# Feed-forward variances as one 512-column product; the inverse deviation by logarithm and exponential on ACT and a Newton step on DVE

## What is computed

```
def ffn_layer(x, g, bln, W1, b1, W2, b2):
    mu = x.mean(-1, keepdims=True)
    var = ((x - mu) ** 2).mean(-1, keepdims=True)
    xn = (x - mu) / jnp.sqrt(var + 1e-05) * g + bln
    hg = xn @ W1 + b1
    a, gate = jnp.split(hg, 2, -1)
    return a * jax.nn.gelu(gate, approximate=False) @ W2 + b2

for i in range(DEPTH):
    x = attn_layer(shift_tokens(x), Wqkv[i], q_scale[i], k_scale[i], Wo[i]) + x
    x = ffn_layer(shift_tokens(x), ln_g[i], ln_b[i], W1[i], b1[i], W2[i], b2[i]) + x
```

## Time and profile before

| | us |
|---|---|
| median of 3 executions (lowest, highest) | 3338.47 (3333.91, 3343.07) |
| the profiled execution, its own time | 3337.87 |
| its span on the core | 3336.1 |

### The profile page before, as it was taken

How to read it: one execution, slowest core, us unless ns; L and a number is a source line. 1 busy time by engine, 2 the same in 40 slices (tenths; PEclk the granted TensorE clock), 3 DMA queues, 4 the chain that set the end, 5 groups by cost and what they waited for, 6 DMA issues and landing times.

```text
span 3336.1 us, 149930 instructions
## 1 busy us (share of the span) xinstructions
PE 3156.5 (95%) x63424; PEld 2622.5 (79%) x63424; DVE 2650.9 (79%) x4403; ACT 2380.2 (71%) x4536; POOL 2592.1 (78%) x2894
## 2 busy tenths in 40 slices
PE   5999999999999999999779999999999999999997
PEld 4888888788888888888668878888888888888875
DVE  3888888888888888888558888888888888888884
ACT  4777777777777777777537777777777777777774
POOL 5987887888788878887349778878887888787773
PEclk8999999999999999999879999999999999999999
DMA  2221222221221222221112222222212212221211
GB/s 82 76 58 51 68 62 55 64 65 52 64 67 53 62 67 55 62 64 51 32 26 75 58 55 67 62 52 68 64 49 67 64 53 65 64 56 50 54 46 40
DMA packets 117857, 195.41 MB, mean 59 GB/s; under 512 B 23756, under 2 KB 36552, under 8 KB 117192
## 3 DMA queue, kind: packets, MB, share of 16 engines
q1 hardware_dynamic: 117192, 185.82, 20.8%
HBM read 33.71 MB, written 1.05 MB: 10 GB/s over the span
## 4 chain that ended last, share of the span: by engine, by line
PE 66%; DVE 13%; ACT 10%; issue 9%; DVEq 0%; ACTq 0%; POOL 0%; DMA 0%; POOLq 0%; SPq 0%
PE s_ps L925 11%; PE tr L969 9%; DVE ss_floor L721 7%; PE tr L938 6%; PE tr L866 5%; PE o_ps L954 4%; PE f_ps L1015 4%; ACT qt L544 4%; PE tr L868 2%; PE tr L867 2%; PE qk_ps L866 2%; PE qk_ps L867 2%; PE qk_ps L868 2%; PE tr L893 2%; PE tr L906 2%
## 5 line engine op out<-in xcount | busy, mean ns | idle before, releaser
L420 POOL TENSOR_TENSOR rotated<-rotated 128x1024 f32<-128x1024 f32 x384 | 916.2, 2386 | 28.8 <-DVE rotated L714 28.8
L426 POOL TENSOR_TENSOR prob<-prob,rden 128x512 f32<-128x512 f32 x384 | 435.7, 1135 | 464.8 <-DVE rden L746 464.2
L449 POOL TENSOR_TENSOR rotated<-rotated,rn 128x1024 f32<-128x1024 f32 x384 | 730.6, 1903 | 30.1
L708 DVE TENSOR_TENSOR rotated<-qk_ps,rot 128x1024 f32<-128x1024 f32 x384 | 470.0, 1224 | 211.7 <-ACT sq L528 208.1
L574 ACT ACTIVATE pt<-tr 128x512 f32<-128x512 f32 x384 | 229.3, 597 | 450.8 <-PE tr L938 450.8
L714 DVE TENSOR_TENSOR rotated<-qk_ps,rot 128x512 f32<-128x512 f32 x768 | 491.0, 681 | 0.0
L925 PEld LDWEIGHTS s_ps<-kt,qt 64*32 64x32 f32 x24576 | 360.8, 107 | 140.4 <-issue 124.4
L721 DVE TENSOR_REDUCE ss_floor<-sq 128x16 f32<-128x1024 f32 x384 | 464.1, 1209 | 0.4
L925 PE MATMUL s_ps<-kt,qt 64*32 64x64 f32 x24576 | 423.2, 218 | 0.3 <-issue 0.2
L528 ACT ACTIVATE sq<-qk_ps 128x1024 f32<-128x1024 f32 x384 | 388.0, 1010 | 26.3 <-PE qk_ps L868 25.7
L969 PE MATMUL tr<-ot,wo 128*128 128x128 f32 x3072 | 406.6, 275 | 0.0
(11 more groups left out here) (152 smaller groups left out, 6968.9 us busy)
## 6 DMA issues: line engine op xcount, KB each, us to landing
vs<-vn SPq DMA_DIRECT2D x384, 192.0 KB, 2.6
vs<-vtail SPq DMA_DIRECT2D x384, 64.0 KB, 2.0
vtail<-vn SPq DMA_DIRECT2D x384, 64.0 KB, 2.3
staging<-layer_wqkv_dram SPq DMA_DIRECT2D x72, 256.0 KB, 3.0
wo<-layer_wo_dram SPq DMA_DIRECT2D x12, 512.0 KB, 3.9
xs<-xa SPq DMA_DIRECT2D x48, 128.0 KB, 2.3
fs<-xa SPq DMA_DIRECT2D x48, 128.0 KB, 2.3
xs<-xa SPq DMA_DIRECT2D x48, 127.8 KB, 2.4
```

The source lines that it names most:

```text
L420: nc.gpsimd.tensor_tensor(rot_c[h], rot_c[h], rot_s[h], ALU.add).then_inc(rot_added, 1)
L426: nc.gpsimd.tensor_tensor(prob[h][:, :, :], prob[h][:, :, :], rden[h][:, :].unsqueeze(2).to_broadcast([P, 2 * PAIRS, KEYS]), ALU.mult).the ...
L449: nc.gpsimd.tensor_tensor(folded, folded, rn[:, :].unsqueeze(2).to_broadcast([P, 2 * UH, DH]), ALU.mult).then_inc(qkn_ready, 1)
L708: nc.vector.tensor_tensor(rot_c[h], src, part(0, 0, DH), ALU.mult)
```

## The change

The variance becomes one product of the 128x128 matrix of 1/128 with the 512 columns of squares, so that every partition holds the variance of every token and nothing has to be spread. ACT takes the logarithm of variance plus epsilon and the exponential of -1/2 of it, and squares this first value; DVE makes one Newton step with it and the scaling in three operations of 512 columns. The factor -0.5 of the step is folded into the copy `fd`. The new ACT work stands at the end of slot 5, the new DVE work in slot 6, and DVE's work of slots 5 and 7, POOL's power and PE's `spread` are gone. The similar code of the layer norm ahead of each stack stays.

```diff
--- before.py
+++ after.py
@@ -141,8 +141,8 @@
         fsq = sb("fsq", [P, SEQ])
         fn_hi = sb("fn_hi", [P, SEQ], F32R)
         fn_lo = sb("fn_lo", [P, SEQ], F32R)
-        var = sb("var", [P, TPS])
-        rstd = sb("rstd", [P, TPS])
+        eps = sb("eps", [P, 1])
+        frsq = sb("frsq", [P, SEQ])
         mac_var = sb("mac_var", [P, SEQS, TPS])
         mac_rstd = sb("mac_rstd", [P, SEQS, TPS])
         gate = [sb(f"gate{i}", [P, HS]) for i in range(3)]
@@ -219,9 +219,11 @@
         fsq_ready = sem("fsq_ready")
         fd_ready = sem("fd_ready")
         fvarp_ready = sem("fvarp_ready")
-        fvar_ready = sem("fvar_ready")
-        frstd_ready = sem("frstd_ready")
-        frb_ready = sem("frb_ready")
+        flog_ready = sem("flog_ready")
+        fguess_ready = sem("fguess_ready")
+        fguess_squared = sem("fguess_squared")
+        fscaled = sem("fscaled")
+        fresidue_ready = sem("fresidue_ready")
         fn_ready = sem("fn_ready")
         fn_hi_ready = sem("fn_hi_ready")
         fn_split = sem("fn_split")
@@ -378,12 +380,13 @@
 
         @block.gpsimd
         def _(pool):
-            for released in (rn_ready, rot_added, qkn_ready, probn_ready, w1_split, frstd_ready):
+            for released in (rn_ready, rot_added, qkn_ready, probn_ready, w1_split):
                 pool.sem_inc(released, ONE)
             for h in range(2):
                 nc.gpsimd.memset(vtail[h][:, :, :], 0.0).then_inc(zeros_ready, 1)
                 nc.gpsimd.memset(kt[h][:, :, :], 0.0).then_inc(zeros_ready, 1)
             nc.gpsimd.memset(three[:, :], 3.0)
+            nc.gpsimd.memset(eps[:, :], EPS)
             nc.gpsimd.memset(ss_floor[:, :, :], SQUARE_FLOOR)
             nc.gpsimd.memset(mean_mat[:, :], 1.0 / P).then_inc(zeros_ready, 1)
             nc.gpsimd.memset(minus_half[:, :], -0.5).then_inc(zeros_ready, 1)
@@ -467,9 +470,6 @@
                     if live(p, n + 1):
                         inverse_norms(n + 1)
                         normalise(n + 1)
-                    if (it := ffn_of(p, n, VAR_AT + 1)) is not None:
-                        pool.wait_ge(fvar_ready, ONE + it + 1)
-                        nc.gpsimd.tensor_tensor(rstd[:, :], var[:, :], minus_half[:, 0:TPS], ALU.pow).then_inc(frstd_ready, 1)
                     g, m = layer_slot(p, n)
                     if m == 11:
                         split_w1(g)
@@ -584,7 +584,16 @@
 
                 act.wait_ge(fcen_ready, ONE + it + 1)
                 nc.scalar.activation(fsq[:, :], f_ps[:, :], ACT.Square).then_inc(fsq_ready, 1)
-                nc.scalar.activation(fd[:, :], f_ps[:, :], ACT.Copy).then_inc(fd_ready, 1)
+                nc.scalar.activation(fd[:, :], f_ps[:, :], ACT.Copy, scale=-0.5).then_inc(fd_ready, 1)
+
+            def inverse_std(it):
+
+                act.wait_ge(fvarp_ready, ONE + it + 1)
+                nc.scalar.activation(fsq[:, :], f_ps[:, :], ACT.Ln, bias=eps[:, :]).then_inc(flog_ready, 1)
+                act.wait_ge(flog_ready, it + 1)
+                nc.scalar.activation(frsq[:, :], fsq[:, :], ACT.Exp, scale=-0.5).then_inc(fguess_ready, 1)
+                act.wait_ge(fguess_ready, it + 1)
+                nc.scalar.activation(fsq[:, :], frsq[:, :], ACT.Square).then_inc(fguess_squared, 1)
 
             def normed_high(it):
                 l = it // SEQS % DEPTH
@@ -642,6 +651,8 @@
                         tokens_high(it)
                     if (it := ffn_of(p, n, MEAN_AT)) is not None:
                         centred(it)
+                    if (it := ffn_of(p, n, VAR_AT + 1)) is not None:
+                        inverse_std(it)
                     if (it := ffn_of(p, n, NORM_AT)) is not None:
                         normed_high(it)
                     if (it := ffn_of(p, n, GATED_AT)) is not None:
@@ -665,7 +676,7 @@
         @block.vector
         def _(dve):
             for released in (summed, ss_ready, rot_parts, max_ready, dif_ready, rden_ready, y_added, xs_split,
-                             fvar_ready, fn_ready, fn_split, hid_ready, xa_ready):
+                             fresidue_ready, fscaled, fn_ready, fn_split, hid_ready, xa_ready):
                 dve.sem_inc(released, ONE)
             dve.wait_ge(consts_in, 48)
             dve.wait_ge(zeros_ready, 8)
@@ -753,14 +764,15 @@
                 cols = xa[:, s, t * P:(t + 1) * P]
                 nc.vector.tensor_tensor(cols, tr0[:, 0:P], cols, ALU.add).then_inc(y_added, 1)
 
-            def variance(it):
-                dve.wait_ge(fvarp_ready, ONE + it + 1)
-                nc.vector.tensor_scalar(var[:, :], f_ps[:, 0:TPS], EPS, None, ALU.add).then_inc(fvar_ready, 1)
-
-            def spread(it):
+            def scale_normed(it):
+
                 l = it // SEQS % DEPTH
-                dve.wait_ge(frb_ready, ONE + it + 1)
-                nc.vector.scalar_tensor_tensor(fd[:, :], fd[:, :], vecs[:, l, 0:1], f_ps[:, :], ALU.mult, ALU.mult).then_inc(fn_ready, 1)
+                dve.wait_ge(fguess_squared, it + 1)
+                nc.vector.scalar_tensor_tensor(fsq[:, :], f_ps[:, :], EPS, fsq[:, :], ALU.add, ALU.mult).then_inc(fresidue_ready, 1)
+                nc.vector.scalar_tensor_tensor(fd[:, :], fd[:, :], vecs[:, l, 0:1], frsq[:, :], ALU.mult, ALU.mult).then_inc(fscaled, 1)
+                dve.wait_ge(fresidue_ready, ONE + it + 1)
+                dve.wait_ge(fscaled, ONE + it + 1)
+                nc.vector.scalar_tensor_tensor(fd[:, :], fsq[:, :], 3.0, fd[:, :], ALU.subtract, ALU.mult).then_inc(fn_ready, 1)
 
             def normed_low(it):
                 l = it // SEQS % DEPTH
@@ -792,10 +804,8 @@
                         prob_sums(n - 1)
                     if (it := staged_for(p, n, 2)) is not None:
                         tokens_low(it)
-                    if (it := ffn_of(p, n, VAR_AT + 1)) is not None:
-                        variance(it)
-                    if (it := ffn_of(p, n, SPREAD_AT + 1)) is not None:
-                        spread(it)
+                    if (it := ffn_of(p, n, SPREAD_AT)) is not None:
+                        scale_normed(it)
                     if (it := ffn_of(p, n, NORM_AT + 1)) is not None:
                         normed_low(it)
                     if (it := ffn_of(p, n, ADD_AT)) is not None:
@@ -829,7 +839,7 @@
         @block.tensor
         def _(pe):
             for released in (qk_ready, v_ready, qtp_ready, ktp_ready, s_ready, ptp_ready, o_ready, y_ready, fcen_ready,
-                             fvarp_ready, frb_ready, gated_ps, fy_ready):
+                             fvarp_ready, gated_ps, fy_ready):
                 pe.sem_inc(released, ONE)
             pe.wait_ge(consts_in, 48)
             pe.wait_ge(consts_ready, 2)
@@ -977,16 +987,7 @@
 
             def variances(it):
                 pe.wait_ge(fd_ready, ONE + it + 1)
-                for c in range(TPS):
-                    last = nc.tensor.matmul(f_ps[:, c:c + 1], fsq[:, c * P:(c + 1) * P], mean_mat[:, 0:1], start=True, stop=True)
-                last.then_inc(fvarp_ready, 1)
-
-            def spread(it):
-                pe.wait_ge(frstd_ready, ONE + it + 1)
-                for c in range(TPS):
-                    last = nc.tensor.matmul(f_ps[:, c * P:(c + 1) * P], rstd[:, c:c + 1].to_broadcast([P, P]), ident[:, :],
-                                            start=True, stop=True)
-                last.then_inc(frb_ready, 1)
+                nc.tensor.matmul(f_ps[:, :], mean_mat[:, :], fsq[:, :], start=True, stop=True).then_inc(fvarp_ready, 1)
 
             def gated(p, n, it):
                 pe.wait_ge(fn_split, ONE + it + 1)
@@ -1042,8 +1043,6 @@
                         centre(it)
                     if (it := ffn_of(p, n, VAR_AT)) is not None:
                         variances(it)
-                    if (it := ffn_of(p, n, SPREAD_AT)) is not None:
-                        spread(it)
                     if (it := ffn_of(p, n, GATED_AT)) is not None:
                         gated(p, n, it)
                 if p == 0:
```

## The result

The changed kernel takes 3402.17 us (median of 4 executions, 3399.34 to 3405.45) against 3336.19 us for the kernel before with all its executions so far. The ratio is 1.0195, with a 95% interval of 1.0175 to 1.0215: slower by 66 us. The prediction had said 3401 us, by the mechanism that follows. The profiled execution has a span of 3398.5 us against 3336.1, 62.4 us more.

A forecast was written before the change was run, and what follows sets the result against it. A 7.10 us ring through PE, DVE and ACT bounds the kernel outside PE's heavy slots. 46 x 1.40 = 64.4, less 1 for the ends, gives +63 on 3337.87: 3401 us, forecast 3388 to 3412 (chance 0.50), 3350 to 3430 (0.81).

The forecast's parts named there:

- The ring of 7.10 us and PE's 6.75: Between V marks (value projection starts on PE): lap through PE, DVE, ACT 7.10 us; PE without feed-forward work 6.75.
- The variance product, slot 4: On PE, one 512-column product for four one-column products: between 0 and +0.07 us, booked as 0.
- ACT, slot 5 to 6: Three new ACT operations delay slot 6's exponential by 1.40 us, making V6 0.77 us late.
- DVE, slot 6 to 7: Three new DVE operations, one held up by POOL, delay the rotation; V6 to V7 takes 8.27 us.
- The blocking of DVE by POOL: Slot 6: DVE's second new operation stands still until POOL's L426 is done, taking about 1.1 us.
- the rival: Slot 6: no meeting of DVE and POOL, V7 +0.93 us, +42 us in all, 3380 us; chance 0.18.
- The steady part: V7 1.40 us late, and the delay stays: 46 x 1.40 = 64.4 us.
- The two ends: Stand-alone last feed-forward behind each stack, at the lower clock: about 5.7 us instead of 6.17, -0.5 us, twice.
- The new work fills idle time: Faster rival: ACT's idle time around slot 5's copy takes the new work; -42 us, 3296 us; chance 0.08.
- Only ACT's delay counts: Rival: DVE catches up in slot 6, V7 +0.23 us, +10 us in all, 3348 us; chance 0.12.
- The third falls behind `normalise`: Rival, slot 6: DVE's third operation loses nearly 1.9 us more to POOL's L449; +147 us, 3485 us; chance 0.04.
- Dearer operations: Rival: logarithm and exponential towards their upper bound, 0.3 to 0.6 us more on the path; 3415 to 3430 us; chance 0.08.

The follow-up runs named there:

- swap: Changed kernel with DVE's first two new operations in the other order, the one with two SBUF inputs first: 3385.04 us, ratio 1.0148.
- psum_step: Changed kernel with DVE's three operations rewritten through the PSUM bank, each reading at most one tile of SBUF: 3386.34 us, ratio 1.0151.
- spread_tokens: Changed kernel with ACT's logarithm and exponential before slot 5's copy, DVE's operations in PSUM form across slots 6 to 8, later feed-forward and token staging: 3304.95 us.
- act_only: Changed kernel without the Newton step: product and ACT's three operations kept, one 512-column DVE operation in slot 7: 3357.60 us, ratio 1.0068.
- neither: Changed kernel with the product only: ACT's three operations and the Newton step left out, inverse deviation a constant 1.0: 3312.57 us, ratio 0.9932.
- tokens_after: Changed kernel with only the token staging moved, ACT's `xs_hi` one slot later and DVE's `xs_lo` two: 3408.68 us, ratio 1.0213.

## Why the prediction was right

The bound. The ring of 7.10 us and PE's 6.75 were read from slots 5 and 6 of one sequence. The run with the product alone shows the ring from V5 to V8, three slots in a row, and rules out that PE's full saving comes out.

The variance product, slot 4: booked at 0 between 0 and +0.07; it was -0.04.

ACT, slot 5 to 6: 0.77 us forecast, 0.86 measured. The logarithm takes 0.68 and not the 0.60 of a copy out of PSUM; the exponential and the square take 0.64 and 0.63, where 0.63 and 0.60 were booked.

DVE, slot 6 to 7: 8.27 forecast, 8.26 measured. Inside, errors offset each other: the second operation took 1.20 instead of 1.12 and the third started 0.11 us behind it instead of 0.04; but the first took 0.64 instead of 0.70, and the third lost nothing to POOL where 0.1 was booked. The blocking of DVE by POOL is the step on which the choice between 3380 and 3401 hung, and both swap and psum_step confirm it: without DVE's wait the kernel is 17 or 16 us faster, where the rival had put 21.

The Trainium skill's rule (SBUF — State Buffer, Who interferes with whom) was the ground for it beside the earlier trace rows. By that rule alone swap should move the waiting from DVE to POOL, and the trace agrees: 0.70 for 1.20 us on DVE, 1.44 for 1.04 on POOL. The other rule of the Trainium skill, to optimise the most-contended engine first (Perfetto Trace Analysis, Identifying the Most-Contended Engine), gives the sign of the product alone (3312.57 us), not its size. For the whole change it gives the wrong sign (3402.17 us).

The steady part was then forecast at 1.40 us and came at 1.44, so 64 and 66 us. The two ends were wrong in sign: -0.5 us each was forecast, +0.24 and +0.23 measured. The failed step is the product's duration there, taken as 1.46 from the centre product; it took 2.07. The granted clock was 0.72 over that centre product (3305.3 to 3306.7 before) and 0.50, the lower level, over the new one (3370.1 to 3372.1), where PE had stood idle for 1.18 us ahead of it. That the total still fits within about 1 us is partly luck. Between the profiled executions the stretch between the stacks gave 4 us back, which the prediction did not have. And between the medians the change costs 66 us, not 63; but the sum stood on 3337.87, and the median before came down to 3336.19 with one more execution.

The side effects: the projection in slot 7 starts 1.08 us behind the output projection (1042.38 to 1043.46) instead of 0.81, which is the 0.2 us booked, ahead of the longer wait of 1.02 for `queries`. And `fn_lo` in slot 0 did become slower (1.11 us on average instead of 0.75) without a cost to the slot, as said. PE's busy time fell by 29 us and not by some 40; no run here separates the reasons.

The rivals fell as follows. "The new work fills idle time" needs gaps at the place where the work is put; there is enough idle time (spread_tokens), but not there. "Only ACT's delay counts" would give 7.10 for slot 6 to 7; it was 8.26. "The third falls behind `normalise`" did not happen: POOL's small operations were themselves held up. "Dearer operations" came to 0.08 us for the logarithm, 0.01 for the exponential and 0.03 for the square.

## What to carry to other kernels

In an in-order pipeline over several engines, follow one lap of the waits and compare it with the busiest engine's own work for that lap: if they are close, work moved off the busiest engine pays only until that engine's time falls to the lap's (here 7.64 - 7.10 = 0.54 of 0.89 us). Work put on the others then lengthens the lap, unless it stands where they already wait. Look for such gaps by place and length (here 1.0 us ahead of one copy on ACT, 0.6 us ahead of one rotation on DVE) and cut the new work to them. Where DVE and POOL run side by side and DVE is on the path, keep one of DVE's two inputs in PSUM, or issue the operation before POOL's: 1.20 us became 0.70 here either way.

## What had not been expected of the hardware

Between the two stacks the same instructions ran at different clock levels in the two profiled executions: the first 16 of the 32 passes that spread the inverse deviations of the stack's layer norm there (L855 before, L865 after) took 3.76 us before and 2.03 after. The granted clock over the 10 us stretches around them was 0.66 (1672 to 1682) and 1.00 (1705 to 1715); PE had been busy 6.62 of the 10 us ahead in both. Over all 13 profiled executions these 16 passes took either 2.03 us (after, act_only, neither, spread_tokens) or 3.76 (the other nine). With the full computation, the time from the centre product behind the first stack to the first one of the second is 159.8 and 160.5 us in the first case and 163.1 to 164.6 in the second. The changed kernel and tokens_after fall into different cases with the same code there, so single executions can differ by some 4 us for no reason in the code. What decides between the two is open.

A DVE operation of 512 columns that writes to PSUM took 0.67 to 0.70 us where the like form writing to SBUF took 0.64 to 0.70, so keeping an intermediate in the bank is close to free. A logarithm of 512 columns, out of PSUM and with a tile for its bias, took 0.68 us on ACT; an exponential or a square in SBUF took 0.63. No run here separates the function from the bias.
